# Attention with a mixture of experts on one core: the projection's place in TensorE's order

## The chip, the cores and the metric

The kernel runs on one core of a Trainium2 chip, as one program. The metric is the device time of one execution in microseconds (us). TensorE (PE in the profile, with its weight loads listed apart as PEld), VectorE (DVE), ScalarE (ACT), GpSimd (POOL) and SyncE (SP) each work through a queue of their own, and wait for each other through counting semaphores.

## The reference, cut to what matters

```python
h = layernorm(x) * (1 + ca) + sa                 # x: 8 batches, 512 tokens, 128 channels, fp32
q, k, v = h @ Wq.T, h @ Wk.T, h @ Wv.T           # 16 heads of 64
q = q / |q| * q_scale;  k = k / |k| * k_scale    # per token and head
attn = softmax(q @ k.T * 64 ** -0.5)             # 512 x 512 per head and batch
x = x + ga * ((attn @ v) @ Wo.T + bo)
h = layernorm(x) * (1 + cb) + sb
x = x + gb * (shared_ffn(h) + experts(h))        # 8 experts, 2 per token, with a capacity
```

The change lies in the attention part: the first six lines, for 8 batches.

## The kernel before, in words

The attention part goes through 64 **slots**: 8 batches (b) times 8 pairs of heads (hp). Slot u = 8 b + hp computes two heads of one batch. It has four steps, called **pairs** (0 to 3), one for each 128 queries. The slots are a software pipeline: while slot u makes its scores, it also projects queries, keys and values for slot u + 2, turns queries and keys for slot u + 1, and weighs values for the slots before. TensorE's order within a slot is the order of the text in `slot` of its block (lines 826 to 854). In each pair it is:

- `project` (L663, matmuls L671 to L673): three accumulating 128x384 matmuls for slot u + 2 and the pair's 128 tokens, into one PSUM bank, `PJ_BANK`. It waits until ScalarE has copied the projection before it out of that bank (`pj_copied`). Slots 62 and 63 have none.
- the turns and the side work, all into the bank `XT_BANK` (which is also `M_BANK`). Pair 0: `between` (L797), which by hp is a part of the output projection (L760 to L762), the turn of normalised rows (L778), of y (L770) or the router (L786). Pair 1: `inverse_rows`, the turn of the inverse row sums (L732). Pair 2: `transpose_q` (L680), the turn of the next slot's queries. Pair 3: `transpose_k` (L687), that of the keys.
- `scores` (L701): six matmuls 64x512, three products for each of two heads, in three banks used in rotation. The scores of pair p wait for the exponential of tile 2p - 2 (`p_done`), those of pair 0 also for the low part of the keys (`kl_done`).
- `transpose_probs` (L721): sixteen 64x64 turns of probabilities into `T2`; pairs 0 and 1 do the slot before.
- `weigh_values` (L745): the weighted sums of a finished slot, two products that run as four matmuls 128x512.

One user of `XT_BANK` follows another only when the one before has been read. The chain of it over pairs 2 and 3 is: `transpose_q`, ScalarE's `high_q` (L899), VectorE's `low_q` (L1039), `transpose_k`, ScalarE's `high_k` (L904), VectorE's `low_k` (L1046, which sets `kl_done`), and then the side work and the scores of the next slot's pair 0. Scores need the high and the low parts both.

ScalarE's order in each pair: `copy_projection` (L890) for slot u + 2, which waits for the pair's projection (`pj_ready`); then a ScalarE part of the side work (pair 0), `copy_inverse` (L921, pair 1), `high_q` (pair 2) or `high_k` (pair 3); in the slots hp 0 and hp 3 also the normalised rows of a layer norm (L358, pair 3); then two `exponentials` (L911), each after VectorE's maximum; then in pairs 1 and 3 a copy of turned probabilities (L916).

VectorE's order in each pair: in pair 0 the inverse of the row sums (L1062), the sums of squares (L1028) and a first guess of norms, and its part of the side work (an added y at L1091, the residual at L1097); in pair 2 `normalise` (L1068); then two `row_max` (L1051), which wait for the scores; then `low_q` (pair 2) or `low_k` (pair 3); in pairs 0 and 2 a copy of turned probabilities (L1057). GpSimd squares the projections (L1255), finishes the norms (L49 to L55, L1265), widens the inverse sums (L1271) and splits the outputs (L1281, L1283). SyncE starts no DMA within the slots.

Of the kernel before, what the change touches and what calls it, by code (L numbers as in the profile page):

```python
# [30 lines left out]
def after(engine, semaphore, value):  # L31

    if not (isinstance(value, int) and value <= 0):
        engine.wait_ge(semaphore, value)
# [26 lines left out]
def adaln_attention_moe(nc, x, Wq, Wk, Wv, Wo, bo, q_scale, k_scale, proj_w, proj_b, expert_bias,  # L61
# [6 lines left out]
    HP = H // 2  # L68
# [9 lines left out]
    with ExitStack() as whole:  # L78
# [212 lines left out]
        with ExitStack() as scope:  # L291
# [308 lines left out]
            def is_const(b, value):  # L600
                return isinstance(b, int) and b == value

            def units_before(b, hp):

                return HP * b + hp if isinstance(b, int) else HP

            def with_next(b, hp, ahead):

                return not (is_const(b, B) or is_const(b, LAST) and hp + ahead >= HP)
# [13 lines left out]
            def s_bank(hp, i):  # L623

                return S_BANK[(S_TILES * hp + i) % 3]
# [22 lines left out]
            with nc.Block() as block:  # L648
# [13 lines left out]
                def _(pe):  # L662
                    def project(w, hp, wb, t, front=None):  # L663

                        if front is not None or hp % HP == 0:
                            pe.wait_ge(hT_ready, NT * wb + t + 1)
                        after(pe, pj_copied, front + 1 - 7 if front is not None else NT * w + t)
                        o = (PJ_BANK if front is None else FRONT_BANKS[front])[:, 0:3 * P].rearrange("p (n c) -> p n c", n=3)
                        cols = slice(hp % HP * P, (hp % HP + 1) * P)
                        toks = slice(t * P, (t + 1) * P)  # L670
                        nc.tensor.matmul(o, hT_h[:, toks], wqkv_h[:, :, cols], start=True, stop=False)  # L671
                        nc.tensor.matmul(o, hT_h[:, toks], wqkv_l[:, :, cols], start=False, stop=False)  # L672
                        nc.tensor.matmul(o, hT_l[:, toks], wqkv_h[:, :, cols], start=False,  # L673
                                         stop=True).then_inc(pj_ready, 1)

                    def transpose_q(w, hp, free):
                        pe.wait_ge(qn_done, 2 * w + 1)
                        after(pe, *free)
                        for t in range(NT):
                            last = nc.tensor.transpose(XT_BANK[:, t * P:(t + 1) * P], qkv[:, hp % 4, t, 0:P], ident[:])  # L680
                        last.then_inc(qt_ready, 1)

                    def transpose_k(w, hp):
                        pe.wait_ge(qn_done, 2 * w + 2)
                        pe.wait_ge(ql_done, w + 1)
                        for t in range(NT):
                            last = nc.tensor.transpose(XT_BANK[:, t * P:(t + 1) * P], qkv[:, hp % 4, t, P:2 * P], ident[:])  # L687
                        last.then_inc(kt_ready, 1)

                    def scores(u, hp, pair):  # L690

                        if pair == 0:
                            pe.wait_ge(kl_done, u + 1)
                        first = S_TILES * hp + 2 * pair
                        after(pe, p_done, S_TILES * u + 2 * pair + (0 if first == 0 else -1))
                        toks = slice(pair * P, (pair + 1) * P)
                        own = parts[:, hp % 2]
                        for q, k in ((QH, KH), (QH, KL), (QL, KH)):
                            for head in range(2):
                                rows = slice(head * DH, (head + 1) * DH)  # L700
                                last = nc.tensor.matmul(s_bank(hp, 2 * pair + head)[:], own[rows, q, toks], own[rows, k],  # L701
                                                        start=((q, k) == (QH, KH)), stop=(q == QL))
                                if q == QL:
                                    last.then_inc(s_ready, 1)
# [21 lines left out]
                    def inverse_rows(u, *free):  # L726

                        pe.wait_ge(wide_done, u + 1)
                        for semaphore, value in free:
                            after(pe, semaphore, value)  # L730
                        for t in range(NT):
                            last = nc.tensor.transpose(XT_BANK[:, t * P:(t + 1) * P],  # L732
                                                       inv_wide[:, t].rearrange("p h d -> p (h d)"), ident[:])
                        last.then_inc(r_ready, 1)
# [62 lines left out]
                    def between(b, hp, u):  # L797

                        free = (kl_done, u + 1)
                        if hp in Y_HP[0:2]:  # L800
                            project_out(b, Y_HP.index(hp), free)
                            return (y_first, b + 1) if hp == Y_HP[0] else (y_more, 3 * b + 1)
                        if hp == H1T_HP and not is_const(b, LAST):
                            transpose_ln(h1_nth(b + 1), free)
                            return (h1_done, b + 2)
                        if is_const(b, 0):
                            if hp in W_HP:
                                j = W_HP.index(hp)
                                transpose_shared(j, free)
                                return (g_low, j + 1)  # L810
                            return free
                        if hp in Y_HP[2:]:
                            project_out(b - 1, Y_HP.index(hp), free)
                            return (y_more, 3 * (b - 1) + Y_HP.index(hp))
                        if hp == YT_HP:
                            transpose_y(b - 1, free)
                            return (x1_done, b)
                        if hp == H2T_HP:
                            transpose_ln(h2_nth(b - 1), free)
                            return (h2_done, b)  # L820
                        if hp == Z_HP:
                            router(b - 1, free)
                            return (z_done, b)
                        return free

                    def slot(b, hp):

                        u = HP * b + hp
                        earlier = units_before(b, hp)
                        side = (kl_done, u + 1)  # L830
                        for pair in range(NT):
                            if with_next(b, hp, 2):
                                project(u + 2, hp + 2, b + (hp + 2) // HP, pair)
                            if pair == 0:
                                side = between(b, hp, u)
                            if pair == 1 and earlier >= 1:
                                inverse_rows(u - 1, side)
                                side = (r_copied, u)
                            if pair == 2 and with_next(b, hp, 1):
                                transpose_q(u + 1, hp + 1, side)  # L840
                            if pair == 3 and with_next(b, hp, 1):
                                transpose_k(u + 1, hp + 1)
                            scores(u, hp, pair)
                            if pair < 2 and earlier >= 1:
                                transpose_probs(u - 1, pair + 2)
                            if pair >= 2:
                                transpose_probs(u, pair - 2)
                            if pair < 2 and earlier >= 2:
                                weigh_values(u - 2, hp - 2, pair + 2)
                            if pair >= 2 and u < END and earlier >= 1:  # L850
                                weigh_values(u - 1, hp - 1, pair - 2)
                            if pair >= 2 and u == END:
                                weigh_values(u - 1, hp - 1, 2 * pair - 4)
                                weigh_values(u - 1, hp - 1, 2 * pair - 3)

                    def batch(b):
                        for hp in range(HP):
                            slot(b, hp)
# [1042 lines left out]
```

## Time and profile before

| | us |
|---|---|
| median of 3 runs | 1296.35 (1296.24 to 1296.62) |
| the profiled execution's own time | 1295.64 |
| its span, first to last instruction | 1293.9 |
| TensorE busy in the span | 1236.8 (96%) |
| VectorE / ScalarE / GpSimd busy | 993.2 / 967.5 / 828.7 |
| mean granted TensorE clock | 0.975 |

The profile is that of one execution. Its busy times are sums of drawn durations, and matmuls are drawn overlapping: six score matmuls are drawn 0.96 us long, and the next group starts 0.80 us after them. So for TensorE the distance from one group's start to the next one's is the time that a group costs, and a short wait can hide inside a share of busy time near 100%. The attention part takes the span from about 22 to 1001 us, the experts the rest.

### The profile page before, as it was taken

To read this page: it belongs to the slowest core of one execution; us is meant where nothing else is said; L and a number is where in the kernel's file an instruction comes from. 1 tells how busy PE (TensorE), PEld (TensorE's weight loads), DVE (VectorE), ACT (ScalarE), POOL (GpSimd) and SP (SyncE) were. 2 spreads that over 40 slices of the span, in tenths; PEclk is the share of its full clock that TensorE was granted. 3 is DMA by queue.
4 is the path that set the end of the run, shared out by engine and by line. 5 is a ranking of instruction groups with operands and counts; after the bars stand their busy time and mean duration, and the time that the engine had idled before them with its cause. 6 is when DMAs were issued, how large, how long until landed. Compare 5 with 4: busy or idle time off the path is not lost. (4 is left out here: it accounts for less than half of the span.)

```text
span 1293.9 us, 28719 instructions
## 1 busy us (share of the span) xinstructions
PE 1236.8 (96%) x9690; PEld 818.5 (63%) x9690; DVE 993.2 (77%) x2048; ACT 967.5 (75%) x2066; POOL 828.7 (64%) x1652
## 2 busy tenths in 40 slices
PE   4799999999999999999999999999999598999997
PEld 4556666666666666666666666666665376788886
DVE  3678777887887887888778877887878775577766
ACT  4677778777777787877788777877787286788886
POOL 2666677767767786777677667766674085344443
PEclk8799999999999999999999999999999699899999
DMA  6000000000000000000000000000000201446451
GB/s 159 2 1 2 1 2 1 2 1 2 2 2 1 2 2 1 2 2 1 2 2 2 2 2 1 2 2 2 1 2 2 68 1 40 92 99 108 100 107 44
DMA packets 36610, 27.99 MB, mean 22 GB/s; under 512 B 8832, under 2 KB 34688, under 8 KB 36480
## 3 DMA queue, kind: packets, MB, share of 16 engines
q1 hardware_dynamic: 35296, 25.92, 9.1%
q8 instruction: 74, 1.21, 0.4%
q10 hardware_dynamic: 1184, 0.40, 0.1%
q14 instruction: 56, 0.46, 0.1%
HBM read 24.09 MB, written 2.23 MB: 20 GB/s over the span
## 5 line engine op out<-in xcount | busy, mean ns | idle before, releaser
L911 ACT ACTIVATE probs<-bank,neg_max 128x512 f32<-128x512 f32 x512 | 347.6, 684 | 212.6 <-DVE neg_max L1051 211.0
L1051 DVE TENSOR_REDUCE neg_max<-bank 128x1 f32<-128x512 f32 x512 | 329.6, 686 | 139.8 <-PE bank L701 137.7
L745 PE MATMUL bank<-probsT,qkv 128*64 128x512 f32 x1024 | 275.1, 617 | 0.3 <-DVE probsT L1211 0.3
L701 PE MATMUL bank<-operands 64*128 64x512 f32 x1536 | 248.4, 428 | 2.2 <-ACT probs L911 1.7
L721 PEld LDWEIGHTS T<-ident,probs 64*128 64x128 f32 x4080 | 167.4, 139 | 47.0 <-issue 21.4
L671 PEld LDWEIGHTS bank<-operands,hT_h 128*128 128x128 f32 x254 | 48.0, 189 | 199.0 <-issue 196.2
L721 PE MATMUL T<-ident,probs 64*128 64x64 f32 x4080 | 170.7, 223 | 2.9 <-issue 1.4
L701 PEld LDWEIGHTS bank<-operands 64*128 64x128 f32 x1536 | 125.2, 185 | 63.8 <-issue 42.3
L1255 POOL TENSOR_TENSOR sq<-qkv 128x256 f32<-128x256 f32 x252 | 150.1, 614 | 15.6 <-ACT qkv L890 15.6
L1057 DVE COPY probsT<-T 128x1024 f32<-128x1024 f32 x128 | 155.6, 1216 | 0.1
L1872 POOL TENSOR_TENSOR hid_l<-act_out,hid_h 128x512 fp32r<-128x512 f32 x64 | 82.8, 1294 | 110.8 <-ACT hid_h L1774 110.8
L1271 POOL TENSOR_TENSOR inv_wide<-inv_sum,consts 128x512 f32<-128x512 f32 x64 | 66.6, 1040 | 130.3 <-DVE inv_sum L1062 130.3
L1265 POOL TENSOR_TENSOR qkv<-qkv,rn 128x512 f32<-128x512 f32 x128 | 131.6, 1049 | 5.0
L890 ACT ACTIVATE qkv<-bank 128x384 f32<-128x384 f32 x254 | 125.2, 494 | 8.3 <-PE bank L673 4.0
L916 ACT ACTIVATE probsT<-T 128x1024 f32<-128x1024 f32 x126 | 128.7, 1022 | 0.0
L671 PE MATMUL bank<-operands,hT_h 128*128 128x384 f32 x254 | 113.2, 446 | 1.5 <-DVE hT_l L1082 1.5
L911 ACT ACTIVATION_READ_ACCUMULATOR probs<-bank,neg_max 128x1 f32 x512 | 100.3, 196 | 0.0
L1788 ACT ACTIVATE act_out<-bank,up_bias 128x512 f32<-128x512 f32 x96 | 66.3, 691 | 28.5 <-PE bank L1716 26.1
L672 PE MATMUL bank<-wqkv_l,hT_h 128*128 128x384 f32 x254 | 87.2, 343 | 0.0
L673 PE MATMUL bank<-operands,hT_l 128*128 128x384 f32 x254 | 87.0, 342 | 0.0
L1805 DVE TENSOR_TENSOR hid_l<-act_out,hid_h 128x512 fp32r<-128x512 f32 x64 | 45.7, 714 | 52.2 <-ACT hid_h L1774 52.2
L1283 POOL TENSOR_TENSOR oT_l<-oT,oT_h 128x512 fp32r<-128x512 f32 x62 | 79.2, 1277 | 4.9
(262 smaller groups left out, 2374.0 us busy)
## 6 DMA issues: line engine op xcount, KB each, us to landing
probsT<-gate_scratch SPq DMA_DIRECT2D x64, 256.0 KB, 4.8
out<-x_all SPq DMA_DIRECT2D x8, 256.0 KB, 4.9
probsT<-in_L_ffn_fc_w SPq DMA_DIRECT2D x1, 1024.0 KB, 8.2
raw<-in_L_attn_Wq SPq DMA_DIRECT2D x1, 512.0 KB, 4.7
raw<-in_L_attn_Wk SPq DMA_DIRECT2D x1, 512.0 KB, 7.5
raw<-in_L_attn_Wv SPq DMA_DIRECT2D x1, 512.0 KB, 8.7
raw_o<-in_L_attn_Wo SPq DMA_DIRECT2D x1, 512.0 KB, 8.7
route<-in_L_ffn_sh_w SPq DMA_DIRECT2D x2, 256.0 KB, 5.5
```

Source lines behind the costliest of these rows:

```text
L671: nc.tensor.matmul(o, hT_h[:, toks], wqkv_h[:, :, cols], start=True, stop=False)
L672: nc.tensor.matmul(o, hT_h[:, toks], wqkv_l[:, :, cols], start=False, stop=False)
L701: last = nc.tensor.matmul(s_bank(hp, 2 * pair + head)[:], own[rows, q, toks], own[rows, k], start=((q, k) == (QH, KH)), stop=(q == QL))
L721: last = nc.tensor.transpose(out[half][:, at:at + DH], probs[rows, (2 * pair + head) % 4, j * P:(j + 1) * P], ident[rows, rows])
L745: last = nc.tensor.matmul(O_BANK[rows, :], qkv[:, hp % 4, j, cols], probsT[:, hp % 2, head, j], start=(j == 0), stop=(j == NT - 1), skip_g ...
L890: nc.scalar.activation(qkv[:, hp % 4, t], bank[:, 0:3 * P], ACT.Copy).then_inc(pj_copied, 1)
L911: nc.scalar.activation(probs[:, i % 4], s_bank(hp, i)[:], ACT.Exp, bias=neg_max[:, i:i + 1], accum_out=row_sum[:, hp % 2, i:i + 1]).then_i ...
L916: nc.scalar.activation(pair_tiles(hp, pair), t_pair, ACT.Copy).then_inc(t_act, 1)
L1051: nc.vector.reduce_max(neg_max[:, i:i + 1], s_bank(hp, i)[:], AX.X, negate=True).then_inc(max_done, 1)
L1057: nc.vector.tensor_copy(pair_tiles(hp, pair), t_pair).then_inc(t_dve, 1)
L1255: nc.gpsimd.tensor_tensor(sq[:, t], qk, qk, ALU.mult).then_inc(sq_done, 1)
L1265: nc.gpsimd.tensor_tensor(rows, rows, by, ALU.mult).then_inc(qn_done, 1)
```

## The change

In TensorE's `slot`, the call of `project` with its condition moves from the start of each pair to the place behind `scores`. Before, a pair is: project, side work or turns, scores, turned probabilities, weighted sums. After it, a pair is: side work or turns, scores, project, turned probabilities, weighted sums. No other queue's program changes. This is the whole diff:

```diff
@@ -829,8 +829,6 @@
                         earlier = units_before(b, hp)
                         side = (kl_done, u + 1)
                         for pair in range(NT):
-                            if with_next(b, hp, 2):
-                                project(u + 2, hp + 2, b + (hp + 2) // HP, pair)
                             if pair == 0:
                                 side = between(b, hp, u)
                             if pair == 1 and earlier >= 1:
@@ -841,6 +839,8 @@
                             if pair == 3 and with_next(b, hp, 1):
                                 transpose_k(u + 1, hp + 1)
                             scores(u, hp, pair)
+                            if with_next(b, hp, 2):
+                                project(u + 2, hp + 2, b + (hp + 2) // HP, pair)
                             if pair < 2 and earlier >= 1:
                                 transpose_probs(u - 1, pair + 2)
                             if pair >= 2:
```

## Rows read from the trace of the kernel before

**Rows 1.** Busy time of each engine in one stretch; then granted clock, DMA share, GB/s.

```profile
500.00:700.00 200.00, 199.55 (x1770) 125.29 (x1769) 161.81 (x312) 154.14 (x353) 143.90 (x326) 1.00 0.01 2
```

**Rows 2.** Timeline, TensorE, one slot: start, duration, line, operation, [idle before].

```profile
613.01 0.44 PE L671 MATMUL bank<-operands,hT_h 128*128 128x384 f32 x1
...
613.64 0.60 PE L732 MATMUL bank<-ident,inv_wide 128*128 128x128 f32 x4
614.17 0.96 PE L701 MATMUL bank<-operands 64*128 64x512 f32 x6
614.97 0.66 PE L721 MATMUL T<-ident,probs 64*128 64x64 f32 x16
615.56 1.08 PE L745 MATMUL bank<-probsT,qkv 128*64 128x512 f32 x4
...
617.73 0.97 PE L701 MATMUL bank<-operands 64*128 64x512 f32 x6
...
620.82 0.63 PE L687 MATMUL bank<-ident,qkv 128*128 128x128 f32 x4
621.37 0.97 PE L701 MATMUL bank<-operands 64*128 64x512 f32 x6
...
625.98 0.96 PE L701 MATMUL bank<-operands 64*128 64x512 f32 x6
```

**Rows 3.** Timeline, VectorE, the same slot and the start of the next.

```profile
618.72 1.29 DVE L1051 TENSOR_REDUCE neg_max<-bank 128x1 f32<-128x512 f32 x2 [1.35 <-PE bank L701]
619.93 0.74 DVE L1039 SCALAR_TENSOR_TENSOR operands<-bank,qk_scale,operands 128x512 fp32r<-128x512 f32 x1
...
624.58 0.20 DVE L1062 RECIPROCAL inv_sum<-row_sum 128x8 f32<-128x8 f32 x1 [0.32 <-ACT probs L911]
...
626.98 1.29 DVE L1051 TENSOR_REDUCE neg_max<-bank 128x1 f32<-128x512 f32 x2
```

**Rows 4.** Timeline, the first slots, where the pipeline fills.

```profile
37.47 0.60 ACT L904 ACTIVATE operands<-bank 128x512 fp32r<-128x512 f32 x1 [2.05 <-PE bank L687]
...
38.10 0.69 DVE L1046 TENSOR_TENSOR operands<-bank,operands 128x512 fp32r<-128x512 f32 x1 [1.90 <-ACT operands L904]
...
38.85 1.65 PE L701 MATMUL bank<-operands 64*128 64x512 f32 x6 [0.45 <-DVE operands L1046]
...
40.43 0.69 PE L671 MATMUL bank<-operands,hT_h 128*128 128x384 f32 x1
...
52.85 0.63 PE L778 MATMUL bank<-ident,h_ln 128*128 128x128 f32 x4 [0.85 <-DVE operands L1046]
```

**Rows 5.** Timeline, ScalarE: the slot of rows 2, and the rows of a layer norm.

```profile
576.77 1.64 ACT L358 ACTIVATE h_ln<-x_all,ln_shift,rstd 128x128 f32<-128x128 f32 x4
...
613.84 0.49 ACT L890 ACTIVATE qkv<-bank 128x384 f32<-128x384 f32 x1
614.27 0.60 ACT L921 ACTIVATE inv_row<-bank 128x512 f32<-128x512 f32 x1
615.89 0.69 ACT L911 ACTIVATE probs<-bank,neg_max 128x512 f32<-128x512 f32 x1 [1.02 <-DVE neg_max L1051]
616.48 0.19 ACT L911 ACTIVATION_READ_ACCUMULATOR probs<-bank,neg_max 128x1 f32 x1
...
618.51 0.70 ACT L899 ACTIVATE operands<-bank,qk_scale 128x512 fp32r<-128x512 f32 x1
```

**Rows 6.** Waits of the weight loads (us in total, times, longest), and two projections in a row.

```profile
PEld bank L671 <- issue: 196.2, 242, 0.8
...
26.38 0.34 PE L671 MATMUL bank<-operands,hT_h 128*128 128x384 f32 x1
...
26.90 0.34 PE L671 MATMUL bank<-operands,hT_h 128*128 128x384 f32 x1
```

**Rows 7.** Timeline, TensorE: the router's matmuls of two batches that follow each other.

```profile
473.40 1.03 PE L786 MATMUL bank<-projT,m_out 128*128 128x8 f32 x8
...
594.06 1.03 PE L786 MATMUL bank<-projT,m_out 128*128 128x8 f32 x8
```

## The prediction

> **What bounds the kernel now.** I read three views. First the busy time of a stretch in the middle of the attention part: TensorE 199.55 of 200 us at a granted clock of 1.00, VectorE 161.81, ScalarE 154.14, GpSimd 143.90 [rows 1]. TensorE looks full, so a reordering can't hide much more there; the question is what it exposes. Second, TensorE's own line over one slot [rows 2]. I take start-to-start times, because drawn durations overlap. One step of a slot (a "pair") is: projection, turns, scores, turned probabilities, weighted sums. Projection to turns is 0.63 (613.01 to 613.64), turns to scores 0.53, scores to turned probabilities 0.80, those to weighted sums 0.59, and the whole pair 3.56 (614.17 to 617.73), which leaves 1.01 for the weighted sums. A pair without turns is 3.03. Third, who sets those times. From the scores of pair 2 to the turns of the keys the reader sees 617.73 to 620.82, that is 3.09, not 3.03. That is a chain through VectorE: row maxima start 0.99 after the scores (618.72), the low part of the queries at 619.93 takes 0.74, and TensorE resumes 0.15 later [rows 2, 3]. So TensorE already waits 0.06 there though its busy share shows nothing. The kernel is bound by TensorE's own work with a chain of the same length right beneath it.
>
> **What the change does.** It only moves project: per slot 4 projections (12 matmuls) go from before the turns to behind the scores, in 62 of the 64 slots. No instruction, byte or DMA is added, and nothing passes SP's or GpSimd's queue. ScalarE's program is not changed: its copy of the projection still stands first in each pair, ahead of the copy of the turned queries or keys and of the exponentials. So the copy now can't start before the scores and the projection are through, and all that queues behind it on ScalarE shifts. That is an added wait, and I price it chain by chain, from the start of the scores (S).
>
> *Cost of each hop.* S to projection: the trace has it only in the first slot, at half clock, 38.85 to 40.43, 1.58 [rows 4]. Half of that is 0.79. If only the columns scale (three rounds of 512, two heads side by side: 1.28 us at 1.2 GHz, 0.64 at 2.4) and 0.30 stays, it is 0.94. I take 0.80, as scores to turned probabilities at full clock [rows 2]; the ends are 0.79 and 0.94. Projection start to copy start: 613.01 to 613.84, 0.83 [rows 2, 5]. Copy to the next operation of ScalarE: 0.43 (613.84 to 614.27) [rows 5].
>
> *Queries (pair 2).* S + 0.80 + 0.83 + 0.43 is the high part of the queries; it takes 0.70 [rows 5]; VectorE follows a ScalarE result after 0.03 (37.47 + 0.60 to 38.10) [rows 4]; its low part takes 0.74, TensorE resumes 0.15 later [rows 3]. Sum 3.68. TensorE itself would be at the turns of the keys at 3.03 (the projection's 0.63 is spent behind the scores). It waits 0.65 where it waited 0.06: **+0.59 per slot**.
>
> *Keys (pair 3).* 0.80 + 0.83 + 0.43 + 0.60 + 0.03 + 0.69 + 0.15 = 3.53 until the next slot's first work, which waits for the low keys; TensorE would be there at 3.03: **+0.50 per slot**. Today it has no wait here, since the projection covered 0.63 of that chain.
>
> *Pairs 0 and 1.* Ring of the exponentials: S + 0.80 + 0.83 + 0.43 + 0.53 (copy of the inverse sums, spacing estimated from its 0.60) starts the first exponential at 2.59, its sum is read 0.78 later (615.89 to 616.48 + 0.19) [rows 5], plus 0.1 to TensorE: 3.47 against 3.56. It fits by 0.09. The maxima start 0.99 after S as now, and the first exponential used to wait for them (615.89 is S + 1.72), so moving scores forward by 0.63 gives ScalarE nothing. Price 0; if this cover is gone, the excess over 0.09 comes twice per slot. The unseen neighbours are projection to turned probabilities (0.63 as to turns; ends 0.52, as one projection follows another [rows 6], and 0.79) and weighted sums to turns (1.01 as to projection; ends 0.86 and 1.16, one gap of 0.15 less or more). They count only in pairs 0 and 1: each -0.15 to +0.16, twice a slot. Price 0, and 62 x 2 x 0.15 = 19 us either way for each.
>
> *Slots with a layer norm.* In 14 slots ScalarE normalises rows (1.64 us [rows 5]) between the high keys and the exponentials of pair 3. The rows are now done at about S + 2.06 + 0.60 + 1.64 = 4.30, TensorE's turn of them at 4.4: 0.9 past 3.53. The slot's last exponential ends near 5.66 (start of the first at 4.2, 0.68 to the second, 0.78 to its end), VectorE then needs some 1.7 to its first maximum (624.58 to 626.98 less the 0.69 of an added y) [rows 3], and the next scores wait about 0.5 more. That is 1.4, but such slots wait already: a batch takes 594.06 - 473.40 = 120.66 [rows 7] where 8 slots of 4 x 3.03 + 3 x 0.53 and the side work (four of 4.61 - 3.03 = 1.58 [rows 2], three of 0.55, one of 1.0) give 118.65. Of those 2.0 us, 0.5 are the 0.06 above, the rest mostly these two slots. I take 0.8 net: 14 x 0.8 = **11**.
>
> *Small ones.* Seven slots in which VectorE adds the residual ahead of its maxima: 0.4 each, **3**. Two slots of batch 0, where VectorE waits for a ScalarE copy that is now behind the projection's copy: 1.4 each, **3**.
>
> *Sum.* 62 x (0.59 + 0.50) = 67.6, and 11 + 3 + 3: about 85 us. The profiled execution took 1295.64 (span 1293.9), the median is 1296.35; 1296 + 85 = **1381**. The part after attention (from about 1001 us) is untouched.
>
> *A rule against a row.* Ahead of the projection the weight load sat idle 0.8 us in 242 cases, 196.2 us together, and began together with its matmul: behind weighted sums nothing is loaded early [rows 6]. The same first load may go early behind the scores; one projection behind another takes 0.52 (26.38 to 26.90), not 0.63. That 0.1 would come off four times a slot (twice in the chains, twice in the pairs): 25 us, 1356. The Trainium skill, "TensorE: Matmul & The Clock Gate", Part 2, says TensorE pulls weight loads ahead of matmuls in flight when the row groups don't conflict or the background buffer is the target; by it the 1356 would be the time.
>
> **The rivals.**
> 1. *Changeovers or the exponentials' ring cost more* (S to projection near 0.94, or the ring over its 0.09): 0.14 x 4 x 62 = 35 us more, about 1410. For: the only row is at half clock; the margin is thin. Against: scores to turned probabilities is 0.80 at full clock.
> 2. *Early weight loads* behind the scores: 1356, as above. Against: the only row of this order, 40.43, has load and matmul starting together.
> 3. *Faster.* The scores start 0.63 earlier after the previous weighted sums, so maxima and exponentials come earlier and today's waits vanish: 8 x 2.0 = 16 us, 1280. Its place is the turn of the keys; it decides if the queries' chain is under 3.03. It needs ScalarE to get at the turned queries before the projection's copy, or a chain 0.65 shorter than its rows; both speak against it.
> 4. *The clock falls* because TensorE now idles. Then four score groups at 1.65 instead of 0.96 cost 2.8 per slot; all slots, over 1550. Against: in the first slots TensorE waited 0.85 ahead of the turns at 52.85 [rows 4], and they took 0.63, the full-speed length of 620.82 [rows 2]; the new waits are no longer.
> That the change does nothing is no rival: the order of TensorE's queue is the text's order.
>
> **Numbers.** Forecast 0.71 (own range 1360 to 1400), rival 1 0.14, rival 2 0.09, rival 3 0.02, rival 4 0.03, and 0.01 for gains and waits that cancel. The range takes in the forecast with the 19 us of the unseen neighbours, rival 2 and most of rival 1: 1352 to 1410. A measurement of this kernel can tell about 0.2% (2.6 us) from no change; slower 0.97, same 0.01, faster 0.02.
>
> **What would show it.** Right: scores of pair 2 to turns of the keys at 3.7 instead of 3.09; scores of pair 3 to the next slot's side work at 3.5; pairs 0 and 1 still 3.56; a slot with 1.58 of side work 16.4 instead of the 15.3 that its steps give now; ScalarE's wait for VectorE ahead of the exponentials (1.02 at 615.89 [rows 5]) mostly gone and a wait of its projection copy for TensorE in its place; TensorE busy under 95% in the middle, clock 1.00; the wait of weight loads ahead of the projection gone from its place behind weighted sums. Wrong: a key-turn gap near 3.1 (rival 3), pairs 0 and 1 above 3.8 (rival 1), or a clock below 1.00.

## The result and the profile after

The changed kernel takes 1410.35 us (1407.95 to 1412.36, 4 runs) against 1296.35: a ratio of 1.0877, interval [1.0859, 1.0895]. That is 114 us slower. The forecast was 1381 with a range up to 1410, so the direction was right and the size too small, by 29 us or a quarter of the loss. The profiled execution took 1411.83, with a span of 1410.1, 116.2 more than before. One version below had two disturbed executions (1563 and 2833 us), so its times are those of a second set of runs.

The busy time of each engine in the same stretch as [rows 1]:

```profile
500.00:700.00 200.00, 190.24 (x1592) 106.57 (x1591) 146.53 (x283) 137.25 (x317) 130.70 (x290) 1.00 0.01 1
```

TensorE now shows 190 of 200 us, at a clock of 1.00, and does 1592 matmuls instead of 1770. The busy share fell by 5% and the work by 10%: the rest of the loss is inside what is drawn as busy. TensorE's timeline over a slot (hp 5) and into the next; the slot of [rows 2] is hp 6, which has the same groups:

```profile
669.51 1.08 PE L745 MATMUL bank<-probsT,qkv 128*64 128x512 f32 x4
670.52 0.66 PE L732 MATMUL bank<-ident,inv_wide 128*128 128x128 f32 x4
671.11 0.96 PE L701 MATMUL bank<-operands 64*128 64x512 f32 x6
672.00 0.44 PE L671 MATMUL bank<-operands,hT_h 128*128 128x384 f32 x1
672.72 0.71 PE L721 MATMUL T<-ident,probs 64*128 64x64 f32 x16
673.36 1.08 PE L745 MATMUL bank<-probsT,qkv 128*64 128x512 f32 x4
...
674.96 0.96 PE L701 MATMUL bank<-operands 64*128 64x512 f32 x6
675.85 0.44 PE L671 MATMUL bank<-operands,hT_h 128*128 128x384 f32 x1
...
678.67 0.63 PE L687 MATMUL bank<-ident,qkv 128*128 128x128 f32 x4 [0.38 <-DVE operands L1039]
679.22 0.96 PE L701 MATMUL bank<-operands 64*128 64x512 f32 x6
...
682.79 0.47 PE L760 MATMUL bank<-oT_h,wo_h 128*128 128x512 f32 x1 [0.23 <-DVE operands L1046]
...
684.35 0.96 PE L701 MATMUL bank<-operands 64*128 64x512 f32 x6
```

Read by starts, scores to scores over pair 1 (671.11 to 674.96) is 3.85, where it was 3.56 and nothing is waited for. Over pair 2 (to 679.22) it is 4.26 for 3.64, over pair 3 (to 684.35) 5.13 for 4.61. The whole slot hp 6 is 17.10 for 15.36.

The two long pairs are the chains. ScalarE and VectorE in the same slot, in order of time:

```profile
676.67 0.49 ACT L890 ACTIVATE qkv<-bank 128x384 f32<-128x384 f32 x1 [0.61 <-PE bank L673]
677.05 0.68 ACT L899 ACTIVATE operands<-bank,qk_scale 128x512 fp32r<-128x512 f32 x1
677.77 0.75 DVE L1039 SCALAR_TENSOR_TENSOR operands<-bank,qk_scale,operands 128x512 fp32r<-128x512 f32 x1
...
680.94 0.49 ACT L890 ACTIVATE qkv<-bank 128x384 f32<-128x384 f32 x1 [1.86 <-PE bank L673]
681.33 0.59 ACT L904 ACTIVATE operands<-bank 128x512 fp32r<-128x512 f32 x1
681.95 0.69 DVE L1046 TENSOR_TENSOR operands<-bank,operands 128x512 fp32r<-128x512 f32 x1 [0.44 <-ACT operands L904]
```

Scores 674.96, projection 675.85, its copy 676.67, high queries 677.05, low queries 677.77, turned keys 678.67: 3.71, forecast 3.68. For the keys 679.22 to 682.79 is 3.57, forecast 3.53. The waits changed hands as forecast (us in total, times, longest). Before:

```profile
ACT probs L911 <- DVE neg_max L1051: 211.0, 220, 2.6
...
PEld T L721 <- issue: 21.4, 51, 1.1
...
ACT qkv L890 <- PE bank L673: 4.0, 9, 2.0
```

After:

```profile
ACT qkv L890 <- PE bank L673: 323.7, 242, 3.7
...
PEld bank L671 <- issue: 91.9, 248, 0.7
...
PEld T L721 <- issue: 63.8, 249, 1.1
...
ACT probs L911 <- DVE neg_max L1051: 19.5, 18, 2.3
```

ScalarE waits for TensorE at the projection's copy, and hardly for the maxima any more. The third line was not forecast: the first weight load of the turned probabilities is now late 249 times, where the kernel before had 51 such waits. It is a part of the 0.29 that pairs 0 and 1 have grown by; the section on the experiments has the rest.

### The profile page after: what moved, and what is told of

The parts are those of the page before. It is cut to its first block and busy times, and to the rows that moved or that the text cites. A ratio compares the mean times of both kernels' runs of the same rounds, so it can differ in the third digit from the quotient of the medians.

```text
span 1410.1 us, 28719 instructions
## 1 busy us (share of the span) xinstructions
PE 1302.9 (92%) x9690; PEld 794.7 (56%) x9690; DVE 995.8 (71%) x2048; ACT 957.8 (68%) x2066; POOL 830.3 (59%) x1652
## 5 line engine op out<-in xcount | busy, mean ns | idle before, releaser
L721 PEld LDWEIGHTS T<-ident,probs 64*128 64x128 f32 x4080 | 148.6, 139 | 64.6 <-issue 63.8
L721 PE MATMUL T<-ident,probs 64*128 64x64 f32 x4080 | 182.7, 229 | 1.3 <-issue 1.3
L911 ACT ACTIVATION_READ_ACCUMULATOR probs<-bank,neg_max 128x1 f32 x512 | 107.1, 209 | 0.0
L671 PEld LDWEIGHTS bank<-operands,hT_h 128*128 128x128 f32 x254 | 48.1, 190 | 93.8 <-issue 91.9
```

The lines of the kernel that those rows point to most:

```text
L721: last = nc.tensor.transpose(out[half][:, at:at + DH], probs[rows, (2 * pair + head) % 4, j * P:(j + 1) * P], ident[rows, rows])
L911: nc.scalar.activation(probs[:, i % 4], s_bank(hp, i)[:], ACT.Exp, bias=neg_max[:, i:i + 1], accum_out=row_sum[:, hp % 2, i:i + 1]).then_i ...
```

## The experiments

All times below are medians; the kernel before was run beside them and took 1295.5 to 1296.1. "Pair" is scores to scores, read from the starts in the middle of the attention part, where the batches repeat each other to a few hundredths of a us; the value given is that of slots without a wait for a layer norm, unless the text says otherwise.

**Part of the change.** The projection goes behind the scores in two of the four pairs only. (A changeover, in the expectations, is the step from one group of matmuls to the next.)

```diff
+                            if pair >= 2 and with_next(b, hp, 2):
+                                project(u + 2, hp + 2, b + (hp + 2) // HP, pair)
...
                             scores(u, hp, pair)
+                            if pair < 2 and with_next(b, hp, 2):
+                                project(u + 2, hp + 2, b + (hp + 2) // HP, pair)
```

> The projection stands behind the scores in pairs 0 and 1 alone; in pairs 2 and 3 it stands ahead of the turns, as before. Theory A (changeovers): TensorE loads weights early only where the work ahead has the same tile shape, so the new order has two late weight loads more per pair (scores to projection 0.89, projection to turned probabilities 0.72, a pair 3.85 instead of 3.56), also where nothing waits. 62 x 2 x 0.29 = 36 us: about 1332. Rival B (chains only: the whole loss comes through the bank of the turns in pairs 2 and 3, and longer steps elsewhere only follow it): about 1297 to 1302, and pairs 0 and 1 at 3.56.

> The kernel with the projection late in pairs 0 and 1, once more, for a clean time: its profiled execution took 1359.95, not the 1332 of theory A, though pairs 0 and 1 were 3.85 as it said. Reading now: 36 us of changeovers, and 0.6 per slot where pair 3 runs into a pair 0 that has no projection in front, against the 3.03 through the row maxima. Expected 1358 to 1362.

The second set of runs gave 1360.85, ratio 1.0496 [1.0481, 1.0511]. Theory A's 1332 was wrong. Its price was right: pair 0 took 3.85. But 631.04 to 634.08 in this timeline shows what had been left out:

```profile
631.04 0.97 PE L701 MATMUL bank<-operands 64*128 64x512 f32 x6
631.84 0.66 PE L721 MATMUL T<-ident,probs 64*128 64x64 f32 x16
632.43 1.08 PE L745 MATMUL bank<-probsT,qkv 128*64 128x512 f32 x4
634.08 1.03 PE L786 MATMUL bank<-projT,m_out 128*128 128x8 f32 x8 [0.57 <-DVE operands L1048]
```

With no projection behind the scores of pair 3 and none at the start of pair 0, TensorE has 2.4 us of work against the 3.03 of the chain through the maxima and the low keys. It waits 0.64 per slot. A slot of 16.52 for 15.36 is some 0.5 of changeovers and this wait.

The opposite edit, pairs 2 and 3 alone:

> The projection stands behind the scores in pairs 2 and 3 alone. Theory A: the chains of queries and keys at their measured 0.62 and 0.52 more per slot, 62 x 1.14 = 71, and some 4 to 8 us from layer norm slots: about 1372 to 1375; with the run of pairs 0 and 1 it adds up to the full change (+114). Pairs 0 and 1 at 3.56. Rival B: nearly the whole loss, 1400 to 1410.

Measured 1370.37, 1.0587 [1.0551, 1.0623]: near theory A's figure, but only in part for its reasons. Pair 2 is 4.27, as in the full change, and pair 0 stays 3.55. Pair 1, which has no projection left, falls to 2.99, and pair 3, which has two, takes 5.39 for 4.61. So the slots hp 6 and hp 7 grew by 0.83 only, and the slots hp 0, 1, 3 and 4, in or next to a layer norm, by 1.4 to 1.8. The two halves don't add up (65 and 74 against 114): each has a seam of its own, where two projections or none fall between two scores.

**The chains taken away.** TensorE's order is that of the change. ScalarE copies the turned operands first.

```diff
-                            if with_next(b, hp, 2):
-                                copy_projection(u + 2, hp + 2, pair)
                             if pair == 0:
...
                                 high_k(u + 1, hp + 1)
+                            if with_next(b, hp, 2):
+                                copy_projection(u + 2, hp + 2, pair)
```

> TensorE's order is that of the changed kernel; on ScalarE the copy of the projection goes behind the copy of the turned inverses, queries or keys (and behind the side work), still ahead of the exponentials. Theory A: the chains shrink to the one through the row maxima (3.09), which is under TensorE's own 3.27 in this order, so TensorE never waits for the turns' bank, but each pair keeps its 0.29: 4 x 3.27 + 3 x 0.58 + side work is 16.4 for a slot with output projection instead of 17.1: about 1366 to 1372. Rival B (chains only): back to 1300 or less. Rival C (the chain's length is in the exponentials, which are still behind the copy): no change, 1405 to 1412.

Measured 1359.74, 1.0503 [1.0459, 1.0547], 6 under theory A and far from both rivals. Pair 2 in this timeline:

```profile
611.15 0.96 PE L701 MATMUL bank<-operands 64*128 64x512 f32 x6
612.04 0.44 PE L671 MATMUL bank<-operands,hT_h 128*128 128x384 f32 x1
612.75 0.72 PE L721 MATMUL T<-ident,probs 64*128 64x64 f32 x16
613.40 1.08 PE L745 MATMUL bank<-probsT,qkv 128*64 128x512 f32 x4
614.41 0.66 PE L687 MATMUL bank<-ident,qkv 128*128 128x128 f32 x4
615.00 0.96 PE L701 MATMUL bank<-operands 64*128 64x512 f32 x6
```

No wait is left here, and pairs 0, 1 and 2 are all 3.85; pair 3 with an output projection is 4.84. (Slots with a layer norm still wait.) This divides the loss: 51 of the 114 us go with the copy's place, and 64 stay with TensorE's order alone. The control has the copy moved and TensorE's order as before:

> TensorE's order is that of the kernel before; only ScalarE's copy of the projection goes behind the turned operands. A control for the runs that move both. Both theories: the projection is ready early here and the queries' low part waits for the row maxima, not for ScalarE, so 1290 to 1300. If it is over 1305, the copy's place has a price of its own and part of the gain of the moved copy was larger than it looked.

Measured 1296.94, 1.0026 [1.0006, 1.0046]. The copy's place by itself is worth next to nothing; it counts only when the projection comes late.

**What the 0.29 is.** Two other places for the projection. First behind the turns (line 842 of the kernel before and what follows; the old call goes):

```diff
                                 transpose_k(u + 1, hp + 1)
+                            if with_next(b, hp, 2):
+                                project(u + 2, hp + 2, b + (hp + 2) // HP, pair)
                             scores(u, hp, pair)
```

> The order is turns or side work, projection, scores, turned probabilities, weighted sums: the projection has moved behind the turns, yet it has work of its own tile shape ahead of it, and turned probabilities have the scores. ScalarE as before. Theory A: no more late weight loads than before, so pairs 0 and 1 stay at 3.56 (to 3.62); but from the scores to the next turns TensorE has only 2.4 us of work, against 3.09 and 3.03 through maxima and low parts: +0.64 twice per slot, 62 x 1.28 = 79: about 1372 to 1378. Rival B (any place but the first of a pair makes the projection costlier by itself): pairs 0 and 1 at 3.7 or more, about 1395 to 1410.

Measured 1354.03, 1.0459 [1.0423, 1.0494], some 20 under the forecast, and its pairs without waits are 3.51, shorter than before. The forecast had 0.64 more for each of the pairs 2 and 3; they grew by 0.53 and 0.50:

```profile
603.93 0.96 PE L701 MATMUL bank<-operands 64*128 64x512 f32 x6
604.73 0.66 PE L721 MATMUL T<-ident,probs 64*128 64x64 f32 x16
605.32 1.08 PE L745 MATMUL bank<-probsT,qkv 128*64 128x512 f32 x4
606.33 0.66 PE L680 MATMUL bank<-ident,qkv 128*128 128x128 f32 x4
606.74 0.42 PE L671 MATMUL bank<-operands,hT_h 128*128 128x384 f32 x1
607.45 0.97 PE L701 MATMUL bank<-operands 64*128 64x512 f32 x6
```

Its loss is in pairs 2 and 3 (4.18 and 5.11), and in two slots of eight (hp 1 and hp 4) also in pair 1 (3.90). Second, between turned probabilities and weighted sums, with the copy late:

```diff
                             if pair >= 2:
                                 transpose_probs(u, pair - 2)
+                            if with_next(b, hp, 2):
+                                project(u + 2, hp + 2, b + (hp + 2) // HP, pair)
                             if pair < 2 and earlier >= 2:
```

(The old call goes here too.)

> The order is turns, scores, turned probabilities, projection, weighted sums, with ScalarE's copy behind the turned operands as in the run with the copy moved. Theory A (changes of tile shape): turned probabilities have their weights early again (scores to them 0.80, they to the next 0.59 to 0.65), while the projection (behind them) and the turns (behind weighted sums) load late: one late load more than before, a pair of 3.70 between 3.56 and 3.85: 4 x 0.145 x 62 = 36, about 1325 to 1335. Rival B (the cost is that of any projection away from the turns): 3.85, 1360. Rival C (only projection right behind scores costs): 3.56, 1296 to 1302.

The time, 1395.97, 1.08 [1.0768, 1.0831], is far over all three. The pairs 0 and 1 without a wait are 3.71, as theory A said. Pair 2 is 4.32:

```profile
609.83 0.97 PE L701 MATMUL bank<-operands 64*128 64x512 f32 x6
...
613.54 0.96 PE L701 MATMUL bank<-operands 64*128 64x512 f32 x6
614.90 0.71 PE L721 MATMUL T<-ident,probs 64*128 64x64 f32 x16 [0.40 <-issue]
```

Here the projection's later end holds ScalarE's exponentials of pair 1, and with them the copy of turned probabilities behind them (613.76 to 614.79), which the next turned probabilities wait for: "issue" in the row hides a wait for ScalarE. The forecast had not followed that queue.

The four orders side by side. A change of tile is where one group's tile (the numbers like 64\*128 behind the names) differs from that of the group ahead:

| order | changes of tile | pair without a wait |
|---|---|---|
| projection, turns, scores, probabilities, sums (before) | 3 | 3.56 |
| turns, projection, scores, probabilities, sums | 3 | 3.51 |
| turns, scores, probabilities, projection, sums | 4 | 3.71 |
| turns, scores, projection, probabilities, sums (the change) | 5 | 3.85 |

Measured from the order of before, one change of tile more costs 0.15 and two more cost 0.29. It is not a clean price: the two orders with three changes differ by 0.05 between themselves, so from the shorter of them the steps would be 0.20 and 0.34. What it looks like, in the kernel before and then in the changed one, the weight load ahead of turned probabilities with its matmuls:

```profile
618.33 0.72 PEld L721 LDWEIGHTS T<-ident,probs 64*128 64x128 f32 x16
...
618.53 0.66 PE L721 MATMUL T<-ident,probs 64*128 64x64 f32 x16
```

```profile
672.71 0.58 PEld L721 LDWEIGHTS T<-ident,probs 64*128 64x128 f32 x16 [0.24 <-issue]
672.72 0.71 PE L721 MATMUL T<-ident,probs 64*128 64x64 f32 x16
```

Behind scores, of the same tile, the load begins 0.20 ahead of its matmuls; behind the projection it begins with them. This holds throughout. From 100 to 950 us, no load after a change of tile begins more than 0.03 ahead of its matmul, in 677 such places of the kernel before and 1005 of the changed one. Of the 450 places of the kernel before where one group follows another of the same tile, 303 have the load over 0.1 ahead. The changed kernel has no such place.

A load can be late for another reason, and then part of the same price is paid. In the run with pairs 2 and 3 alone, the turned probabilities of one pair 1 (hp 3) stand behind scores, but must wait for VectorE's copy (done at 611.97):

```profile
610.75 1.22 DVE L1059 COPY probsT<-T 128x1024 f32<-128x1024 f32 x1
...
611.16 0.96 PE L701 MATMUL bank<-operands 64*128 64x512 f32 x6
612.04 0.61 PEld L721 LDWEIGHTS T<-ident,probs 64*128 64x128 f32 x16 [0.35 <-issue]
612.07 0.72 PE L721 MATMUL T<-ident,probs 64*128 64x64 f32 x16
612.71 1.08 PE L745 MATMUL bank<-probsT,qkv 128*64 128x512 f32 x4
```

Turned probabilities to weighted sums is 0.64 here too, where it is 0.59 when the load is early. So a late first load makes its group longer even without a change of tile. That the tile is what makes it late in the changed kernel, and not something else that goes with these orders, rests on the counts and the four orders; no run changed a tile by itself.

**Versions meant to beat both.** If turns first is slow by its chains alone, VectorE can free them: the low parts go ahead of the maxima (as here), or between them. TensorE's turns come first and ScalarE's copy late in both.

```diff
                         for pair in range(NT):
...
+                            if pair == 2 and with_next(b, hp, 1):
+                                low_q(u + 1, hp + 1)
+                            if pair == 3 and with_next(b, hp, 1):
+                                low_k(u + 1, hp + 1)
                             row_max(u, hp, 2 * pair)
                             row_max(u, hp, 2 * pair + 1)
-                            if pair == 2 and with_next(b, hp, 1):
-                                low_q(u + 1, hp + 1)
-                            if pair == 3 and with_next(b, hp, 1):
-                                low_k(u + 1, hp + 1)
```

> TensorE: turns, projection, scores, turned probabilities, weighted sums. ScalarE: copy of the projection behind the turned operands. VectorE: the low parts of queries and keys ahead of the pair's two row maxima. If the run with the turns first was slow by its chains alone, both chains (turns, high part, low part) now end near 2.1 after the scores against TensorE's own 2.4, and a pair costs 3.51: a batch of 118 to 119.5 instead of 120.66, about 1276 to 1288, faster than both kernels. Rival: the maxima, held up by the low parts until 1.9 after the scores, push the exponentials so far that the ring of exponentials (3.53) or the copies of turned probabilities set the pair: 1296 to 1320.

> As the run with the low parts ahead of the maxima, but with each low part between the two maxima of its pair. The chains end at 2.5 after the scores, 0.1 past TensorE's 2.4, and the first exponential of the pair is on time: 0.1 to 0.15 twice per slot, 8 to 16 us over the version with the low parts first if that one's exponentials do not bind, 1284 to 1300; below it if they do.

Measured 1304.49, 1.0092 [1.006, 1.0124], and 1305.21, 1.0086 [1.0053, 1.0119]. The first forecast, faster than both kernels, was wrong, and its rival's range held; the second time lies over its range. The freed chains did what they were to do: 50 us of the loss with turns first are gone, plain slots fell under those of before (15.18 and 15.14 for 15.36). But the slots near a layer norm grew: with the low parts first, hp 1 and hp 3 take 15.90 and 15.84, for 15.64 and 14.75. What they wait for was not looked at. Three attempts to take the gain without the loss: the low parts between the maxima with TensorE's order as before; turns first with all that goes with it under the condition `hp in (2, 6, 7)`; and the first of these under a condition too:

```diff
                             row_max(u, hp, 2 * pair)
+                            if hp in (2, 5, 6, 7) and pair == 2 and with_next(b, hp, 1):
+                                low_q(u + 1, hp + 1)
+                            if hp in (2, 5, 6, 7) and pair == 3 and with_next(b, hp, 1):
+                                low_k(u + 1, hp + 1)
                             row_max(u, hp, 2 * pair + 1)
...
```

(In the other slots the low parts stay behind the second maximum.)

> The kernel before, with VectorE's low part of queries and keys between the pair's two row maxima instead of behind them. The keys' turn then no longer waits for the second maximum (3.09 after the scores): scores to scores over pair 2 falls from 3.64 to 3.56 or so in each slot, up to 62 x 0.08 = 5 us: 1290 to 1296. Rival: the second maximum is 0.7 later, with it the second exponential and ScalarE's copies, and turned probabilities wait: 1297 to 1310.

> The order turns, projection, scores, turned probabilities, weighted sums (with the copy behind the turned operands and the low parts between the maxima) in the slots hp 2, 6 and 7 alone, where it was 0.18 to 0.22 shorter than before (15.14 for 15.36, 14.16 for 14.34); the old order in the other five. 8 x 0.6 = 5 us: 1288 to 1294. Rival: the seams between the two orders, or the slots after them, give it back: 1295 to 1300.

> The kernel before, with the low parts between the two row maxima in the slots hp 2, 5, 6 and 7 alone. Over all slots this gave 0.12 to 0.17 in hp 2, 6 and 7 and 0.41 in hp 5, and lost 0.25 to 0.51 in hp 1, 3 and 4, next to the layer norm's rows. Expected 0.12 + 0.41 + 0.17 + 0.13 = 0.8 per batch, 8 x 0.8 = 6.6 us: 1288 to 1292, faster than both kernels. Rival: the gain of hp 5 is only a wait that moves on to the next slots: 1293 to 1297.

They gave 1294.54, 0.9994 [0.9982, 1.0006]; 1300.26, 1.0041 [1.0026, 1.0056]; and 1295.93, 0.9995 [0.998, 1.001]. The first lies in its forecast but can't be told from no change; the second is at the top of its rival's range, and the third within that of its rival. In the last, hp 5 is 15.19 for 15.60 and hp 2, 6 and 7 gain 0.12 to 0.15, but hp 1 and hp 3, whose code is that of before, take 15.87 for 15.64 and 15.30 for 14.75. The gain in some slots comes back as a loss in those next to the layer norms. No version here beats the kernel before.

## Why the prediction was right and wrong

- **The chains: right in length, in part by luck.** Hops summed to 3.68 and 3.53, measured 3.71 and 3.57; per slot +0.62 and +0.52, forecast 0.59 and 0.50. Two hops missed and nearly cancelled: scores to projection is 0.89 to 0.90 (taken as 0.80), and the projection's copy to the next operation of ScalarE 0.38 (taken as 0.43). What fills the time differs too. With the copy moved, pairs 2 and 3 are still 3.85 and 4.84, so 0.20 and 0.23 of the growth are TensorE's own longer order, and 0.42 and 0.29 are the wait, where the prediction had wait alone. Moving the copy takes 51 us back from the changed kernel, so the added wait of ScalarE's queue is a cause, by experiment, at 51 us and not at the 68 of the sum.
- **Pairs 0 and 1, "price 0": the step that failed.** They cost 0.29 to 0.30 each, 62 x 0.59 = 37 us. Scores to projection was 0.89 (taken as 0.80), projection to turned probabilities 0.72 (0.63), these to the sums 0.64 (0.59), turns to scores 0.59 (0.53); the sums stayed at 1.01. The first two lie within the ends that had been named; the last two had been given no ends at all. The mistake was to take every one at its friendly value, and to widen the range for one of them only, as if they were independent. They moved together: each of the four leads to, or starts from, a group whose first load isn't early in this order. The rows gave a hint, but no price: [rows 6] show one transition with a late load.
- **The rule against the row.** The prediction took from the Trainium skill ("TensorE: Matmul & The Clock Gate", Part 2) a time of 1356, with the weights of the projection loaded early behind the scores. The Trainium skill makes such an early load depend on row groups that don't conflict or on the background buffer, and no row here shows whether either held. Early it was not: the projection's load begins with its matmul and is still waited for (91.9 us in 248 cases), and two other groups, the turned probabilities and the turns, lost their early load. In these runs a load is early only behind a group of the same tile.
- **Layer norm slots: 11 + 3 forecast, about 3 measured.** Slot hp 2 grew by 1.76. Slots hp 0 and hp 3 grew by 0.9 and 0.5 more, but hp 1, 4 and 5 by 1.0 less together, since their waits of before (pairs of 3.80 to 3.88) went into the longer pairs: 0.4 per batch. The 0.5 forecast for the scores that follow didn't come: pairs 0 and 1 are 3.87 and 3.85 there as well.
- **The first slot.** In the profiled execution it takes 20.52 (38.92 to 59.44) for 14.55, 4 more than a later slot's growth. The granted clock is at its low level of 1.2 GHz there, in the kernel before until 46 us and in the changed one until 56.4, and once more from 59.8 to 63.3 (mean from 20 to 60 us 0.63 for 0.76). The last slow scores of this stretch in the changed kernel, and the first fast ones in the kernel before:

```profile
53.19 1.65 PE L701 MATMUL bank<-operands 64*128 64x512 f32 x6
```

```profile
46.16 0.96 PE L701 MATMUL bank<-operands 64*128 64x512 f32 x6
```

TensorE's waits in this slot are longer than before (up to 1.79 for 0.90). That they kept the clock low is not shown. So rival 4, the low clock, was real at the start, where the prediction had argued that the new waits would be no longer; in the middle the clock stayed at 1.00.
- **The sum as it is:** 61 x 1.73 = 106, first slot 6, layer norms 3: 115, against 114 (median) and 116 (span). The other seven slots of batch 0 grew by 13.4 together, 1.3 more than 7 x 1.73, with 0.7 over 1.73 in each of hp 2 and hp 4; 3 had been forecast for two slots of this batch.
- **The rivals.** Number 1 named 1410 and was the nearest, for half of its reasons: the changeovers did cost more, the exponentials' ring did not bind. By its own terms it comes to 1381 + 35 = 1416, so part of the match is a slip of the sum. Its sign, pairs 0 and 1 above 3.8, is the one that came. With 0.14 its place in the odds was too low. Numbers 2 and 3 fell: the key turns came 3.71 after the scores, not 3.1 or less.

## What to carry to other kernels

In an in-order queue the item to look at is not the one that is moved but the first one on another engine that waits for it, and all that stands behind that. Then count the places on TensorE where the tile changes from one group to the next: in the order with two more of them per pair, TensorE's order alone cost 64 us here, and the waits 51. And prices that rest on the same unseen thing belong together at one end of the range, not each in its middle.

## What the runs showed that was not expected

A first weight load is early only behind a group of the same tile. Pairs with one and two more changes of tile than before are 0.15 and 0.29 us longer, while TensorE is drawn as busy throughout. Taking a projection out of a gap can cost as much as lengthening a chain: 0.64 per slot where none stood between pair 3 and pair 0. And a projection behind the turns follows them after 0.41 us, where turns to scores take 0.53: so turns first has the shortest pair of all, 3.51. No version here made a whole batch faster with it.
